# Experts of two stages computed on sorted tokens instead of on all tokens, with stages and chunks shared out anew among three lanes

## The reference

```python
logits = jnp.einsum('th,eh->te', x, router_w)              # stage 5
topk_logits, topk_idx = jax.lax.top_k(logits, K)           # K = 2 of E = 8
hmid = jax.nn.gelu(jnp.einsum('th,efh->etf', x, w1) + b1[:, None, :], approximate=False)   # 256 wide
y = jnp.einsum('etf,ehf->eth', hmid, w2) + b2[:, None, :]
out = jnp.einsum('eth,te->th', y, combine)                 # combine is 0 for 6 of 8 experts
...
eo = jnp.einsum('eti,eih->eth', jax.nn.silu(hg) * hu, wd)  # stage 7: 176 wide, 8 experts, 2 used
shared = jax.nn.silu(xf @ swg) * (xf @ swu) @ swd          # stage 7: 352 wide, every token
```

## Time and profile before

| what | value |
|---|---|
| time, median of 3 runs | 1315.03 us (1312.03 to 1319.26) |
| the profiled execution, first to last instruction | 1314.2 us, 0.8 us below that median |
| granted PE clock, mean | 0.975 |
| PE busy | 1262.0 us, 96% of the span |
| DVE, ACT, POOL busy | 927.8, 901.5, 777.6 us |
| moved by DMA | 66.74 MB, mean 51 GB/s |

### The profile page before, as it was taken

The page is one execution under the profiler, slowest core; times in us unless marked ns, Lnnn a source line. Parts: engine busy times, 40 slices in busy tenths (PEclk is TensorE's granted clock), DMA queues, the critical chain, the costliest instruction groups (busy, mean ns, idle before and its releaser), DMA issues.

```text
span 1314.2 us, 25939 instructions
## 1 busy us (share of the span) xinstructions
PE 1262.0 (96%) x8634; PEld 888.8 (68%) x8634; DVE 927.8 (71%) x3613; ACT 901.5 (69%) x2507; POOL 777.6 (59%) x853
## 2 busy tenths in 40 slices
PE   8799689999998999999999999999999999999997
PEld 4355356668744777777776777777788877776665
DVE  5979988867768788767656454787597678655254
ACT  6848899968574898766867666376778758765231
POOL 2989987668457867575655855356524524433434
PEclk9769989999998999999999999999999999999999
DMA  8753000110061000111000101101200011002430
GB/s 284 203 131 95 9 1 2 58 58 2 1 197 34 1 2 2 58 73 30 37 2 2 65 1 68 65 2 66 84 3 2 1 62 29 1 1 66 112 98 24
DMA packets 26373, 66.74 MB, mean 51 GB/s; under 512 B 2945, under 2 KB 7809, under 8 KB 25473
## 3 DMA queue, kind: packets, MB, share of 16 engines
q1 hardware_dynamic: 26240, 65.10, 16.4%
HBM read 61.74 MB, written 3.34 MB: 50 GB/s over the span
## 4 chain that ended last, share of the span: by engine, by line
PE 82%; DVE 9%; ACT 4%; POOL 2%; issue 2%; POOLq 0%; DVEq 0%; ACTq 0%
PE bank L1216 71%; PE bank L1220 11%; DVE arena L2126 2%; ACT arena L1668 2%; DVE arena L1935 2%; ACT L1668 1%; DVE stats L1949 1%; DVE arena L2192 1%; DVE stats L1938 1%; POOL arena L2566 1%; ACT bank L1668 1%; DVE arena L2190 1%; ACT X L1668 0%; POOL stats L2489 0%; DVE arena L2204 0%
## 5 line engine op out<-in xcount | busy, mean ns | idle before, releaser
L1668 ACT ACTIVATE arena<-arena 128x256 f32<-128x256 f32 (+4 forms) x804 | 355.6, 447 | 31.8 <-DVE arena L2192 15.0
L1668 ACT ACTIVATE arena<-bank 128x512 f32<-128x512 f32 (+3 forms) x354 | 190.9, 570 | 199.4 <-PE bank L1216 125.0
L1216 PE MATMUL bank<-XT,W 128*128 128x512 f32 (+1 forms) x720 | 287.5, 534 | 0.4 <-DVE arena L2204 0.3
L1216 PEld LDWEIGHTS bank<-W,arena 128*128 128x128 f32 x1888 | 230.2, 193 | 41.1 <-issue 35.7
L2513 POOL TENSOR_TENSOR arena<-arena 128x512 f32<-128x512 f32 (+2 forms) x108 | 171.3, 1600 | 137.5 <-DVE arena L1935 55.1
L1216 PE MATMUL bank<-W,arena 128*128 128x128 f32 (+1 forms) x1888 | 239.1, 277 | 1.1 <-POOL arena L2513 0.7
L1216 PE MATMUL bank<-arena 128*32 128x128 f32 (+8 forms) x2864 | 222.2, 335 | 6.9 <-DVE arena L2192 4.1
L2565 POOL TENSOR_TENSOR arena<-arena 128x256 f32<-128x256 f32 x192 | 118.6, 618 | 169.6 <-DVE arena L2198 169.1
L2566 POOL TENSOR_TENSOR arena<-arena 128x512 f32<-128x512 f32 x192 | 201.0, 1047 | 0.0
L1216 PEld LDWEIGHTS bank<-arena 128*32 128x32 f32 (+4 forms) x2864 | 147.0, 151 | 79.6 <-issue 52.8
L1220 PE MATMUL bank<-CF,arena 128*128 128x128 f32 x1312 | 181.7, 277 | 8.7 <-POOL arena L2566 5.3
(11 more groups left out here) (153 smaller groups left out, 1693.6 us busy)
## 6 DMA issues: line engine op xcount, KB each, us to landing
arena<-rws SPq DMA_DIRECT2D x44, 512.0 KB, 5.7
arena<-rep SPq DMA_DIRECT2D x62, 256.0 KB, 5.4
arena<-rws SPq DMA_DIRECT2D x8, 384.0 KB, 10.9
W<-w SPq DMA_DIRECT2D x1, 2692.0 KB, 9.1
W<-w SPq DMA_DIRECT2D x1, 2316.0 KB, 8.3
W<-w SPq DMA_DIRECT2D x1, 2124.0 KB, 8.8
XT<-wkq SPq DMA_DIRECT2D x4, 512.0 KB, 5.1
W<-w SPq DMA_DIRECT2D x1, 2005.0 KB, 15.0
```

What stands on the lines that cost most here:

```text
L1216: return e.matmul(o, lhsT, rhs, start=start, stop=stop, skip_group_check=True)
L1668: return e.activation(o, a, func, **kw)
```

## The change

Stage 1 stays dense. In stages 5 and 7 each chunk's tokens are sorted by expert, and each expert works on its own tokens alone. 512 tokens with two experts each make 1024 rows; every expert's rows are rounded up to slabs of 128, which fit into 15 slabs whatever the routing is (`SLABS`). The steps of a task, in the order in which each needs the one before:

- "k": PE counts the tokens before each token by expert (two products with 32 columns), and 19 small DVE operations make of it each token's two row numbers (`index`) and each slab's expert (`expert_ids`). "w" makes the two shares.
- "xc": POOL issues 8 indirect DMAs, each of which scatters 128 tokens (64 KB) to their rows in DRAM (`xsd`). "xs": SP reads the sorted rows back in two DMAs, when all 8 have landed.
- "wl", 15 times: SP loads a slab's expert number into a register and fetches that expert's weights (`experts`, 321 or 320 KB) into a ring of 8 places (`RING`).
- for each of 4 groups n of up to 4 slabs: "xt" transposes the slabs, "up" and "dn" are the two sides of the expert's network on 128 tokens at a time, and "ys" writes the group's result to DRAM (`ysd`).
- "ga": POOL issues 8 indirect DMAs that gather each token's two results. "e": 8 DVE operations multiply them by the shares and add them to the input.
- in stage 7 the shared expert is two steps of its own, "sh" and "so".

The steps wt, ew, er, gw and bb are gone in both stages, and with them the resident weights of both (`W` is smaller, and stage 7's load waits for stage 1 now). `TASKS` is dealt out anew: before, lanes 0 and 1 had 8 tasks and lane 2 had 16; now 10, 10 and 12. `TURNS` is a new table for all 8 stages, so the order of instructions differs on all engines.

```diff
-ROUTED = (1, 5, 7)
-LANE = {0: 0, 1: 1, 2: 2, 3: 2}
+EXPERTS = 8
+SLABS = {5: (2 * CH + 127 * EXPERTS) // 128, 7: (2 * CH + 127 * EXPERTS) // 128}
+SLOTS = 128 * SLABS[5]
...
+    def own_experts():
+
+        add(f"{s}.k", 0, (f"{s}.r", 0))
+        add(f"{s}.w", 0, (f"{s}.k", 0))
+        add(f"{s}.xc", 0, (f"{s}.k", 0), ("xz", c, PREP, 1))
+        for n in range(2):
+            add(f"{s}.xs", n, (f"{s}.xc", 0))
+        for b in range(SLABS[s]):
+            add(f"{s}.wl", b, (f"{s}.k", 0), *([(f"{s}.dn", (b - RING) // 4)] if b >= RING else [("7.so", 0)] if s == 7 and b >= 5 else []))
+        for n in range(4):
+            add(f"{s}.xt", n, (f"{s}.xs", n // 2))
+            add(f"{s}.up", n, (f"{s}.xt", n), *[(f"{s}.wl", b) for b in members(s, n)], *([(f"{s}.dn", n - 2)] if n >= 2 else []))
+            add(f"{s}.dn", n, (f"{s}.up", n))
+            add(f"{s}.ys", n, (f"{s}.dn", n))
+        if s == 7:
+            for n in range(len(WIDE)):
+                add("7.sh", n)
+            add("7.so", 0, ("7.xc", 0), *[("7.sh", n) for n in range(len(WIDE))])
+        add(f"{s}.ga", 0, *[(f"{s}.ys", n) for n in range(4)])
+        add(f"{s}.e", 0, (f"{s}.ga", 0), (f"{s}.w", 0), *([("7.so", 0)] if s == 7 else []))
...
-TASKS = [[(s, 0) for s in range(8)], [(s, 1) for s in range(8)],
-         [(s, c) for c in (2, 3) for s in range(4)] + [(s, c) for s in range(4, 8) for c in (2, 3)]]
+TASKS = [[(s, 0) for s in range(6)] + [(4, 3), (5, 3), (6, 0), (7, 0)],
+         [(s, 1) for s in range(8)] + [(6, 3), (7, 3)],
+         [(s, c) for c in (2, 3) for s in range(4)] + [(s, 2) for s in range(4, 8)]]
+LANE = {task: lane for lane, tasks in enumerate(TASKS) for task in tasks}
...
-OVER = {4: (0,), 5: (1,), 6: (4,), 7: (3, 5)}
+OVER = {4: (0,), 6: (4,), 7: (1,)}
...
-                        e.dma_start(w[:, j * 128:(j + 1) * 128], turned(s, c)[32 * j:32 * j + 8, :]).then_inc(d_ew[c], 16)
+                        e.dma_start(rws[c][:, j * 128:(j + 1) * 128], turned(c)[32 * j:32 * j + 8, :]).then_inc(d_ew[LANE[1, c]], 16)
...
+                elif name in ("5.xs", "7.xs"):
+                    m = len(members(s, 2 * n)) + len(members(s, 2 * n + 1))
+                    on.wait_ge(d_xc[LANE[s, c]], 128 * rounds(s, c))
+                    e.dma_start(raw(c, 2 * n, m).rearrange("p (b d) -> p b d", d=128),
+                                xsd[c][n * 1024:n * 1024 + m * 128, :].rearrange("(b p) d -> p b d", p=128)).then_inc(d_xs[LANE[s, c]][n], 16)
+                elif name in ("5.wl", "7.wl"):
...
+                    which = e.value_load(expert_ids(c)[:, n:n + 1], min_val=0, max_val=EXPERTS - 1)
+                    e.dma_start(fetched(s, c, n), experts[s][bass.ds(which, 1), :, :].rearrange("a p n -> (a p) n")).then_inc(landed(s, c, n // 4)[0], 16)
+                elif name in ("5.ys", "7.ys"):
+                    m = len(members(s, n))
+                    on.wait_ge(*emptied(u("T", f"{s}.dn", c, n)))
+                    e.dma_start(ysd[c][n * 512:n * 512 + m * 128, :].rearrange("(b p) d -> p b d", p=128),
+                                columns(c, n, m).rearrange("p (b d) -> p b d", d=128)).then_inc(d_ys[LANE[s, c]], 16)
...
+                elif name in ("5.k", "7.k"):
+                    b, ps = first(name, c)
+                    on.wait_ge(*after("mk", name, c))
+                    mm(ps[:, 0:32], cst("low"), scratch(c, 152, 32))
+                    mm(ps[:, 32:64], cst("stm")[:, 128:256], scratch(c, 152, 32)).then_inc(full[b.i], 1)
+                elif name in ("5.xt", "7.xt"):
+                    b, m = u("T", name, c, n), len(members(s, n))
+                    on.wait_ge(*free(b))
+                    on.wait_ge(d_xs[LANE[s, c]][n // 2], 16 * rounds(s, c))
+                    transposes(b, [raw(c, n)[:, i * 128:(i + 1) * 128] for i in range(m)])
+                elif name in ("5.up", "7.up"):
+                    (b, ps), (b2, ps2) = first(name, c, n), second(name, c, n)
+                    xt = columns(c, n)
+                    on.wait_ge(*emptied(u("T", f"{s}.xt", c, n)))
+                    for i, k in enumerate(members(s, n)):
+                        on.wait_ge(*landed(s, c, n))
+                        ins = mm(ps[:, i * 128:(i + 1) * 128], fetched(s, c, k, 0, 128), xt[:, i * 128:(i + 1) * 128])
+                    ins.then_inc(full[b.i], 1)
+                    for i, k in enumerate(members(s, n)):
+                        ins = mm(ps2[:, i * 128:(i + 1) * 128], fetched(s, c, k, 128, 128), xt[:, i * 128:(i + 1) * 128])
+                    ins.then_inc(full[b2.i], 1)
...
+                elif name in ("5.dn", "7.dn"):
+                    b, hid, more = u("T", name, c, n), raw(c, n), second_half(c, n)
+                    on.wait_ge(*free(b))
...
+                    for i, k in enumerate(members(s, n)):
+                        ps = bank[b.i][:, i * 128:(i + 1) * 128]
+                        ins = mm(ps, hid[:, i * 128:(i + 1) * 128], fetched(s, c, k, {5: 256, 7: 384}[s], 128), True, False)
+                        if s == 5:
+                            ins = mm(ps, more[:, i * 128:(i + 1) * 128], fetched(s, c, k, 384, 128), False, True)
+                        else:
+                            ins = mm(ps, more[:, i * 128:(i + 1) * 128], fetched(s, c, k, 512, 128), False, True)
+                    ins.then_inc(full[b.i], 1)
...
+                    own(reduce(e8(200), count.rearrange("p (e j) -> p e j", j=4), ALU.add))
+                    on.wait_ge(*own.last())
+                    own(tt(ej(304), e8(200).unsqueeze(2).to_broadcast([128, 8, 4]), cst("th").unsqueeze(1).to_broadcast([128, 8, 4]), ALU.is_gt))
+                    on.wait_ge(*own.last())
+                    own(reduce(e8(184), ej(304), ALU.add))
+                    own(e.tensor_tensor_scan(scratch(c, 208, 32), cst("jm"), count, 0.0, ALU.mult, ALU.add))
...
+                    own(ts(index(c)[:, 0:4], scratch(c, 336, 4), -FAR, None, ALU.add))
+                    e.tensor_copy(index(c)[:, 4:8], scratch(c, 340, 4)).then_inc(has["idx"], 1)
...
+                    own(reduce(scratch(c, 481, 15)[0:1, 0:m], under, ALU.add))
+                    on.wait_ge(*own.last())
+                    e.tensor_copy(expert_ids(c)[:, 0:m], scratch(c, 481, 15)[0:1, 0:m]).then_inc(has["eid"], 1)
...
+                elif name in ("5.e", "7.e"):
+                    to, res = s3(c, 1), rows(s, c)
+                    on.wait_ge(*after("w", f"{s}.w", c))
+                    if s == 7:
+                        on.wait_ge(*emptied(u("b", "7.so", c)))
+                    on.wait_ge(d_ga[LANE[s, c]], 128 * rounds(s, c))
+                    for j in range(4):
+                        js = slice(j * 128, (j + 1) * 128)
+                        own(stt(to[:, js], gathered(c, j), scratch(c, 344 + j, 1), res[:, js], ALU.mult, ALU.add))
+                    on.wait_ge(*own.last())
+                    for j in range(4):
+                        js = slice(j * 128, (j + 1) * 128)
+                        own(stt(to[:, js], gathered(c, 4 + j), scratch(c, 348 + j, 1), to[:, js], ALU.mult, ALU.add))
...
-                elif name in ("1.gw", "5.gw", "7.gw"):
-                    h, k = hidden(s, c, n), n - SHARED[s]
-                    w = shares_at(s, c)[:, k * 512:(k + 1) * 512]
...
+                elif name in ("5.xc", "7.xc"):
+                    src = rows(s, c)
...
+                    for k in range(2):
+                        for j in range(4):
+                            e.indirect_dma_start(xsd[c], bass.IndirectOffsetOnAxis(index(c)[:, 4 * k + j:4 * k + j + 1], 0), src[:, j * 128:(j + 1) * 128], None
+                                                 ).then_inc(d_xc[LANE[s, c]], 16)
+                elif name in ("5.ga", "7.ga"):
+                    on.wait_ge(d_ys[LANE[s, c]], 64 * rounds(s, c))
+                    for k in range(8):
+                        e.indirect_dma_start(gathered(c, k), None, ysd[c], bass.IndirectOffsetOnAxis(index(c)[:, k:k + 1], 0)).then_inc(d_ga[LANE[s, c]], 16)
```

472 lines of the change are left out of this document (323 added, 149 removed), and 510 rows, old and new, of tables (EMITS, OPENS, PARTS, TURNS).

## The result

The changed kernel takes 1399.95 us (median of four runs, 1398.83 to 1403.04) against 1317.14 for the kernel before on the same chip: 1.0646 times as long, 95% interval 1.0614 to 1.0678. The prediction was 1265 us, range 1236 to 1308, so it was wrong in sign. The profiled execution has a span of 1396.9 us against 1314.2, and a mean granted clock of 0.918 against 0.975.

What follows compares the result with a forecast made beforehand. PE was taken as the bound, saturated from 500 to 1250 us. 1314.2 - 94.9 = 1219.3, plus waits 21 and 9.5 and the end 14.9, gave 1264.7 us; 0.8 more for the median, 1265.5; range 1236 to 1308.

Steps and rivals of the forecast that it cites:

- PE work removed: Stages 5 and 7 on PE: fewer 512-column products against more small products and transposes, net -94.9 us.
- the price that would have overturned it: PE's 128-column products with freshly fetched weights in stages 5 and 7: assumed to start 0.22 us apart.
- The rule that was weighed against it: Weight-load busy time measures PE better: 75% in the saturated stretch; if only that came back, near 1290 us.
- Waits: New PE stalls in stages 5 and 7: Wait A 21 us plus Wait B 9.5 us.
- The end: After the last product: copy, write, gathers, landing and combination replace the add, 14.9 us more (9.4 to 30).
- The step that failed: Costed at nothing: POOL loses some 137 us of multiplications, gains 129 us of DMAs; SP's fetches mostly hidden.
- Wait A: From k to the first xt in each (stage, chunk) task: 18.3 us, partly covered; 21 us of PE stalls.
- Wait B: From the last dn to f: 20.8 us, uncovered only at stage 5, chunk 1; 9.5 us (4 to 22).
- Rival 1: Scatter and gather dear on POOL: slower beyond 1.6 us each, 1354 us at 2.1; chance 0.11.
- Rival 2: Scatters and gathers cheap on POOL, at most 0.6 us each: 1238 to 1250 us; chance 0.17.
- Rival 3: Two lanes can't fill PE while the third waits, or reads come late: 1282 to 1308 us; chance 0.21.

Runs made afterwards that it cites:

- m6: m3 plus a small POOL power behind each DMA, so that a batch lasts 9.7 us as in the changed kernel; 1338.11 us.
- m3: Changed kernel with POOL's 128 indirect DMAs replaced by ordinary POOL DMAs of the same bytes, tokens not sorted; 1315.7 us.
- m15: Changed kernel, whole, with a one-column POOL power behind the second, fourth and sixth indirect DMA of each batch; 1359.89 us.
- m2: Changed kernel with each slab's expert number a constant instead of a register load, so wrong weights are fetched; 1382.67 us.
- m7: m3 with constant expert numbers instead of register loads, neither sorted nor routed; 1301.65 us.
- m1: Stand-alone kernel, PE products beside other engines' DMAs or copies; 40 groups take 36.8 us beside scatters, 35.7 alone.
- m8: m3 with the first 1270 turns of the table as in the kernel before; 1311.2 us.
- m16: m15 with a table of turns searched for its batch of 11.6 us; 1344.8 us.

## Why the prediction was wrong

**The sum, term by term.** From one step's start on PE to the next, less the price of that step (the same prices before and after), PE's wait comes out by stretch, in us. The prices are those of the full clock, so what the lower clock costs stands in the waits; the last row estimates that part, as half of the time in which PE was busy while the granted clock was 0.5 (53.8, 158.4, 136.2 and 104.1 us in the four traces). The first 9 us or so stand in no row.

```
                  before   after      m6      m3
work by prices    1185.7  1091.4  1091.4  1091.4
waits 0-500         86.6   105.4   106.1   108.1
waits 500-800       10.0    39.1    26.5    23.7
waits 800-1000       9.0    61.4    43.4    38.5
waits 1000-end       6.7    60.5    26.0    18.7
waits, sum         112.4   266.4   201.9   189.0
of it clock, est.   26.9    79.2    68.1    52.1
last product      1307.0  1367.1  1302.5  1289.7
```

- **PE work removed**: predicted -94.9, counted in the traces at the same prices 1091.4 - 1185.7 = -94.3. The counts are right, and at the full clock so is the price that would have overturned it: eight products of 128 columns from 607.08 to the next start 608.87, 0.224 each against 0.2225. PE's busy time fell by 33.9 us only, 1262.0 to 1228.1 and not to 1167. With the estimated clock part taken off both it falls by 86, 1235.1 to 1148.9, and m6 and m3 come to 1142 and 1145: so some 52 of the 61 us that are missing are products at 1.2 GHz. The rule that was weighed against it (the Trainium skill, Perfetto Trace Analysis, Identifying the Most-Contended Engine), read so that three quarters or 71 us come back, isn't borne out by that 86, which is itself an estimate.
- **Waits**: predicted 21 + 9.5 = 30.5 more, measured 154.0 more. This term failed. 64.5 of it are gone in m6 (266.4 - 201.9) and 12.9 more in m3. Of the 154.0 some 52 are no waiting at all but products at the lower clock (79.2 - 26.9), 11 of them inside the 64.5.
- **The end**: predicted +14.9 (22 us without PE), measured 29.8 us against 7.2, +22.6; m3 has 21.6.
- **Sum**: -94.3 + 154.0 + 22.6 = 82.3, and the spans differ by 82.7.

**The step that failed** is that a POOL DMA costs its time on POOL and nothing else ("POOL loses [...] and gains 128 DMAs [...]: even"; fetches on SP "hidden by the scatters while one costs less than 1.4 us of the queue"). The price of 1.01 us was right as busy time, 0.97 measured; with the gap the spacing is 1.27. While they run, PE's signals and SP's steps are held, about 60 us of the 1400 (m6 and m15 agree), and no term or rival had that. A fetch beside scatters costs 21.4/8 = 2.7 us, so the seven ahead of a sorted read are not hidden; even alone a fetch by register costs 1.1 us, and m2 and m7 put 14 to 17 us on it.

A second step failed with it: the sum takes every product at the full clock, although it adds waits, and no term prices the clock. Over these traces the lower clock grows with the waits (54, 104, 136, 158 us of PE's work in it; waits of 112, 189, 202, 266), also without late signals. In m3, with nearly the time of the kernel before, it is some 25 us of the added 76.6. No run holds the clock and changes the waits, so what each gives the other is not shown.

**Wait A by task**, PE idle from k to the first xt, us (windows):

```
             (5,0) (5,1) (5,3) (5,2) (7,1) (7,2) (7,3) (7,0)
predicted     6.9   0     8.7   0.5   4.8   0.3   0     0
after         8.5   3.6  16.7  11.4   7.6   6.7   6.9   6.8
m6            7.5   1.5   7.7   2.6   4.7   3.2   3.2   3.6
m3            6.8   0     8.1   2.3   3.8   2.6   2.6   3.4
```

With signals on time the three large stalls stand where they were put, within 1 us. Part of that is luck: the prediction's 6.9 at (5,0) has eight scatters of 8.1 us as its longest part, but m3's batch takes 4.4, and what ends its wait is the sorted read, issued behind seven fetches of 7.0 us; and in the wait of (5,3) PE is busy 16.65 us at a mean clock of 0.58 (14.36 at 0.70 in m6) with work priced at 9.6, which makes the idle part smaller. At (5,2) the prediction's own terms give 18.3 - 17.2 = 1.1, not 0.5. The term was mis-sized at the tasks that I put at zero: some 3 us each, even with short batches. (5,3) and (5,2) wait side by side (859.0 to 892.3 and 866.9 to 901.4), so that neither has the other's work for cover; the 11.4 holds part of the 16.7.

**Wait B**: PE idle from the last dn of (5,1) to k of (5,3) is 12.9 us, 8.7 in m6, 6.6 in m3, against 9.5. Right in place and near in size; late signals add 4.2. Another 5.9 us follow ahead of k of (5,2); they lie in the wait of (5,3) above.

**Rivals.** Rival 1 (dear on POOL) had the sign, not the mechanism: its threshold was 1.6 us for each DMA, and 1.27 was measured. What it drew on from the Trainium skill (SBUF — State Buffer, the trap "DVE blocks DMA") hardly shows: beside DVE's copies from SBUF to SBUF in m1 a scatter takes 1.08 us and behind them 0.96, far from 3.1, and in the kernel, with DVE busy 70% of the span, they keep 0.95 to 0.98. Rival 2 (cheap) is out. Rival 3 (lanes) holds in part: without late signals and with short batches m3 still waits 46 us more than the 30.5 that waits A and B were to give (189.0 - 112.4 - 30.5), 21.5 of it before 500 us, where the tasks didn't change. Some 25 of the 46 are the lower clock, 13 of them before 500 us (an estimate, as above). The early order costs only some 4.5 us at the end (m8). A searched table gave 15 (m16). The rest is not separated between order and lanes; the new sharing of lanes was not tried by itself.

**What stays open**: why indirect DMAs hold PE's signals and SP's steps. That they do beside products of 128 columns, from which spacing on, and what it costs here is shown; the mechanism is not, nor why signals beside products of 512 columns kept their time. Each run here has a span and a granted clock from the profiler's records, so none shows whether signals are late where nothing is recorded.
